# The second context is split on VectorE, and SyncE issues constants, two contexts and the first keys ahead of its loop

## The chip, the cores and the metric

The kernel runs on one core of one Trainium2 chip. The metric is device microseconds of one execution, lower is better. Times are shown as the median of several executions of the same program.

## The reference, cut to what matters

Sixteen independent batches of 128 rows by 256 columns go through two cross attentions and two feed-forward blocks. Keys and values of both attentions are the same array, the context.

```python
x = x + _L0_xattn_ref(_layernorm(x), ctx, ctx)      # 16 heads of 16, causal, 128 queries by 128 keys
x = x + _L0_ffn_ref(_layernorm(x), base_w, base_b, router_w, router_b, lora_A, lora_B)
x = x + _L1_xattn_ref(_layernorm(x), ctx, ctx, gamma)  # 8 heads over the columns, 256 by 256
x = x + _L1_ffn_ref(_layernorm(x), w1, w2, gamma)    # two quantised 256x1024 products, GELU between
```

## The kernel before, in words

The kernel is a software pipeline over the 16 batches. A batch b passes numbered stages, and iteration t of an engine does stage s of batch t - s. Every engine has its own order of stages within an iteration: `fill` for t below 8, `body` for t up to 15 (from 14 on in a hardware loop), `drain` after. The engines meet at semaphores only, and each engine, the DMA-issuing SyncE too, works strictly in its written order, so that a wait holds all that stands behind it.

Scores are computed in bf16 with float32 accuracy. For this every context b is split into high, middle and low bf16 parts in the one buffer `k_split` (four instructions: cast of the high part written twice, subtract into `k_rest`, cast of the middle part, subtract of the low part; each counts `k_split_step` up by one, four to a batch). SyncE stores `k_split` to DRAM (`k_parts`, 512 KB, `store_k`, L655), waits until that has landed (`k_parts_out`), and loads it back in another layout into `k0` (`load_k0`, two DMAs, L616 and L617). The normalised x is split and turned in the same way: ScalarE normalises, GpSimd makes the three parts (`q0_rest`, `q0_mid`, `q0_low`), TensorE transposes (`turn_q0`, L1284), ScalarE copies to `q0_t` (`copy_q0`, L1568), SyncE stores (`store_q0`, L664, 256 KB) and loads (`load_q0`, L616 and L617). TensorE then computes the scores (L1104, L1108), VectorE takes the row maxima (L1801), these are split, transposed, copied and stored by SyncE as two more rows of `q0` (`rows0`, L728), and TensorE computes the transposed scores with the maximum subtracted (L1122, L1126), from which ScalarE takes the exponential.

Context 0 is split by VectorE ahead of its iterations (`split_k0`, L2156 to L2160), all others by GpSimd (`k_high` through the helper at L817, `k_rest_` L833, `k_mid` L817, `k_low` L848). `k_high` of batch b stands in GpSimd's iteration b + 1, ahead of `q0_low` of that iteration, and waits until the keys of batch b - 1 have landed in DRAM.

SyncE's order in the first iterations: `load_x` groups 0 and 1 (L599); t = 0: `load_kv(0)` (L634), `store_q0(0)`; t = 1: `load_kv(1)`, `store_k(0)`, `load_q0(0)`, `load_k0(0)`, `store_q0(1)`; t = 2: `load_kv(2)`, `store_k(1)`, `load_q0(1)`, `rows0(0)`, `load_k0(1)`, `store_q0(2)`; t = 3 the same with all batches one further. ScalarE issues the other groups of x and, at the end of its iteration 2, six constants (L1676): the feed-forward weights `wff_sb` (392 KB), four vectors repeated to all partitions (128, 128, 4 and 0.5 KB) and `lora_b_sb` (128 KB). They are first needed by `x1b_`, `ff` and `logits_` of batch 0.

Of the kernel before, what the change touches and what calls it, by code (L numbers as in the profile page):

```python
# [22 lines left out]
ALU = mybir.AluOpType  # L23
# [4 lines left out]
P = 128  # L28
D = 256
# [28 lines left out]
K_LO, K_HI, K_AGAIN, K_MI = range(SLOTS)  # L58
# [136 lines left out]


X_ITERATIONS = {0: 2, 1: 3, 3: 4, 5: 5}
W_FF_ITERATION = 2
W_LOADS = {4: 0, 6: 1}
W_BATCH = 9 - FF  # L200

# [24 lines left out]
def later(b, n):  # L226

    return not isinstance(b, int) or b >= n


def bank_of(order, user):
# [49 lines left out]
def program(nc, x, kv, w_ff, base_b, router_b, lora_b, attn_gamma, w1, w2, mlp_gamma, out):  # L281
    with ExitStack() as ctx:
# [25 lines left out]
        wff_sb = sb("wff_sb", [P, FT, NFF])  # L308
        lora_b_sb = sb("lora_b_sb", [ER, D])
        base_b_all = sb("base_b_all", [P, D])  # L310
        router_b_all = sb("router_b_all", [P, NE])
        attn_gamma_all = sb("attn_gamma_all", [P, 1])
        mlp_gamma_all = sb("mlp_gamma_all", [P, D])
# [10 lines left out]
        kv_in = sb("kv_in", [P, 2, 2, D])  # L324
        v1_in = sb("v1_in", [P, 2, D])
        k_split = sb("k_split", [P, 2, SLOTS, D], BF16)
        k_rest = sb("k_rest", [P, 2, D])
# [235 lines left out]
        def iterations(engine, fill, body, drain):  # L563
            held.clear()
            for t in range(0, FILL):
                fill(t, t % 2)
            for t in range(FILL, LOOP[0]):
                body(t, t % 2)
            with engine.Fori(0, (LOOP[1] - LOOP[0]) // 2) as turn:
                body(turn * 2 + LOOP[0], LOOP[0] % 2)  # L570
                body(turn * 2 + (LOOP[0] + 1), (LOOP[0] + 1) % 2)
            for order, banks in ((S_BANKS, 2), (ST_BANKS, 2), (T_BANK, 1), (U_BANK, 1), (UT_BANK, 1)):
                for n in range(banks):
                    user, stage = [u for m, u in enumerate(order) if m % banks == n][-1]
                    held[(order[0][0], n)] = ((freed[user], NB - stage),)
            for t in range(LOOP[1], END):
                drain(t, t % 2)
# [17 lines left out]
        def load_x(engine, n):  # L595
            first, end = X_GROUPS[n]
            if n > 2:
                engine.wait_ge(x_late_landed, (n - 2) * 16)
            engine.dma_start(xs[:, first * D:end * D].rearrange("p (b d) -> p b d", d=D),  # L599
                             x[first:end].rearrange("b p d -> p b d")).then_inc(x_landed[n] if n < 2 else x_late_landed, 16)  # L600

        def plain(engine):

            engine.sem_inc(waited, 1)
# [16 lines left out]
        def _(sp):  # L621
            def load_kv(t, odd):
                b, odd = at(t, LOAD_KV), (odd + LOAD_KV) % 2
                if b is None:
                    return
                if later(b, 2):
                    split, placed, landed = b * 4 - 4, b - 1, b * 16 - 16
                    sp.wait_ge(k_split_step, split)
                    plain(sp)
                    sp.wait_ge(v0_placed, placed)  # L630
                    plain(sp)
                    sp.wait_ge(kv_landed, landed)
                    plain(sp)
                sp.dma_start(kv_in[:, odd, :, :], kv[b]).then_inc(kv_landed if later(b, 1) else kv0_landed, 16)  # L634

            def load_v1(t, odd):
                b, odd = at(t, LOAD_V1), (odd + LOAD_V1) % 2
# [10 lines left out]

            def store_k(t):
                b = at(t, STORE_K)  # L650
                if b is None:
                    return
                sp.wait_ge(k_split_step, b * 4 + 4)
                plain(sp)
                sp.dma_start(k_parts[b].rearrange("l p c -> p l c"),  # L655
                             k_split[:, :, :, :].rearrange("p l t c -> p l (t c)")).then_inc(k_parts_out, 16)

# [127 lines left out]
                store_out(t)  # L785

            load_x(sp, 0)
            load_x(sp, 1)
            iterations(sp, fill, body, drain)
            sp.wait_ge(stored, NB * 16)  # L790

# [2 lines left out]
        def _(pool):  # L794
# [23 lines left out]

            def k_high(t, odd):
                b, odd = at(t, K_HIGH), (odd + K_HIGH) % 2  # L820
                if b is None or isinstance(b, int) and b == 0:
                    return
                pool.wait_ge(kv_landed, b * 16)
                pool.wait_ge(k_parts_out, b * 16)
                cast(k_split[:, :, K_HI:K_AGAIN + 1, :],
                     kv_in[:, odd, :, :].unsqueeze(2).broadcast_to([P, 2, 2, D])).then_inc(k_split_step, 1)

            def k_rest_(t, odd):
                b, odd = at(t, K_REST), (odd + K_REST) % 2
                if b is None or isinstance(b, int) and b == 0:  # L830
                    return
                pool.wait_ge(k_split_step, b * 4 + 1)
                pool.tensor_tensor(k_rest[:, :, :], kv_in[:, odd, :, :], k_split[:, :, K_HI, :],  # L833
                                   ALU.subtract).then_inc(k_split_step, 1)

            def k_mid(t):
                b = at(t, K_MID)
                if b is None or isinstance(b, int) and b == 0:
                    return
                pool.wait_ge(k_split_step, b * 4 + 2)  # L840
                cast(k_split[:, :, K_MI, :], k_rest[:, :, :]).then_inc(k_split_step, 1)

            def k_low(t):
                b = at(t, K_LOW)
                if b is None or isinstance(b, int) and b == 0:
                    return
                pool.wait_ge(k_split_step, b * 4 + 3)
                pool.tensor_tensor(k_split[:, :, K_LO, :], k_rest[:, :, :], k_split[:, :, K_MI, :],  # L848
                                   ALU.subtract).then_inc(k_split_step, 1)
# [639 lines left out]
        def _(act):  # L1489
# [151 lines left out]
            def fill(t, odd):  # L1641
                exp1(t, 1)
                norm2_high(t)
                copy_max0(t)
                exp1(t, 5)
                exp2(t)
                copy_max1(t)
                copy_u0(t)
                norm2(t)
                exp1(t, 4)  # L1650
                copy_gated(t)
                exp0(t, 1)
                exp1(t, 6)
                exp0(t, 2)
                copy_q0(t)
                norm1(t)
                exp1(t, 2)
                copy_xh1(t)
                exp1(t, 0)
                norm0(t)  # L1660
                norm0_high(t)
                exp0(t, 3)
                copy_u1(t)
                exp1(t, 3)
                exp0(t, 0)
                exp1(t, 7)
                if t in X_ITERATIONS:
                    load_x(act, X_ITERATIONS[t])
                if t == W_FF_ITERATION:
                    for dst, src in ((base_b_all[:, :], base_b.partition_broadcast(P)),  # L1670
                                     (wff_sb[:, :, :], w_ff.rearrange("(k p) n -> p k n", p=P)),
                                     (lora_b_sb[:, :], lora_b),
                                     (router_b_all[:, :], router_b.partition_broadcast(P)),
                                     (attn_gamma_all[:, :], attn_gamma.partition_broadcast(P)),
                                     (mlp_gamma_all[:, :], mlp_gamma.partition_broadcast(P))):
                        act.dma_start(dst, src).then_inc(weights_in, 16)  # L1676
                if t in W_LOADS:
                    load_weight(W_LOADS[t])

# [119 lines left out]
        def _(dve):  # L1799
# [349 lines left out]
                if isinstance(t, int) and t == 13:  # L2149
                    clip_weight(1, (w1_q, w2_q)[1], (w1_sb, w2_sb)[1])  # L2150

            def split_k0():

                dve.wait_ge(kv0_landed, 16)
                step = Steps(dve, k_split_step, 0, 4)
                step.done(dve.tensor_copy(k_split[:, :, K_HI:K_AGAIN + 1, :],  # L2156
                                          kv_in[:, 0, :, :].unsqueeze(2).broadcast_to([P, 2, 2, D]))).wait()
                step.done(dve.tensor_tensor(k_rest[:, :, :], kv_in[:, 0, :, :], k_split[:, :, K_HI, :], ALU.subtract)).wait()
                step.done(dve.tensor_copy(k_split[:, :, K_MI, :], k_rest[:, :, :])).wait()
                step.done(dve.tensor_tensor(k_split[:, :, K_LO, :], k_rest[:, :, :], k_split[:, :, K_MI, :], ALU.subtract))  # L2160

# [2 lines left out]
                dve.memset(tile[:], 0.0).then_inc(prepared, 1)  # L2164
            dve.memset(v0[:, :, :, :], 1.0).then_inc(prepared, 1)
            stats0_group(0)
            split_k0()
            stats0_group(1)
            dve.memset(k0[STK:STM, :, :].bitcast(F32), ONES_BF16).then_inc(prepared, 1)
            dve.memset(v1[:, :, :], 1.0).then_inc(prepared, 1)  # L2170
            stats0_group(2)
            def stats3_(t):
                b = at(t, STATS3)
                if b is None:
# [168 lines left out]
```

## Time and profile before

| | |
|---|---|
| median of 3 runs | 412.84 us |
| lowest, highest | 410.18, 413.76 us |
| the profiled execution's own time | 415.81 us |
| its span from first to last instruction | 413.4 us |
| busy share of PE, DVE, ACT, POOL | 77%, 74%, 64%, 56% |

PE is TensorE, DVE VectorE, ACT ScalarE, POOL GpSimd, SP SyncE; a q behind the name is the engine's sequencer, which issues DMAs. All positions below are microseconds from the start of the profiled execution's span. The profiled execution lies 2.97 us above the median, and its span 2.4 us below its own time.

### The profile page before, as it was taken

To read this page: it belongs to the slowest core of one execution; us is meant where nothing else is said; L and a number is where in the kernel's file an instruction comes from. 1 tells how busy PE (TensorE), PEld (TensorE's weight loads), DVE (VectorE), ACT (ScalarE), POOL (GpSimd) and SP (SyncE) were. 2 spreads that over 40 slices of the span, in tenths; PEclk is the share of its full clock that TensorE was granted. 3 is DMA by queue.
4 is the path that set the end of the run, shared out by engine and by line. 5 is a ranking of instruction groups with operands and counts; after the bars stand their busy time and mean duration, and the time that the engine had idled before them with its cause. 6 is when DMAs were issued, how large, how long until landed. Compare 5 with 4: busy or idle time off the path is not lost.

```text
span 413.4 us, 9678 instructions
## 1 busy us (share of the span) xinstructions
PE 318.2 (77%) x3010; PEld 192.7 (47%) x3010; DVE 307.9 (74%) x838; ACT 264.4 (64%) x501; POOL 230.9 (56%) x449
## 2 busy tenths in 40 slices
PE   0047366497799899999999999999787578566883
PEld 0024244264465465665655665665443234234453
DVE  6432362759899687889997978897885574999983
ACT  2124153355577488789777876777465347988993
POOL 6257465838585557769656676235424113566534
PEclk9996796888899899999999999999996789999999
DMA  3675774976655738658757577623413400001111
GB/s 101 203 210 131 223 212 105 271 204 168 169 152 172 219 86 237 187 167 225 201 159 212 147 209 193 166 57 92 108 57 94 90 2 1 2 17 36 39 52 63
DMA packets 73137, 56.20 MB, mean 136 GB/s; under 512 B 5376, under 2 KB 62592, under 8 KB 73088
## 3 DMA queue, kind: packets, MB, share of 16 engines
q1 hardware_dynamic: 68896, 50.87, 44.8%
q10 hardware_dynamic: 4192, 4.73, 4.5%
q8 instruction: 24, 0.39, 0.5%
q14 instruction: 25, 0.20, 0.2%
HBM read 36.45 MB, written 18.87 MB: 134 GB/s over the span
## 4 chain that ended last, share of the span: by engine, by line
PE 45%; DMA 16%; DVE 12%; issue 9%; ACT 8%; SPq 6%; POOL 3%; ACTq 0%; POOLq 0%; DVEq 0%
DMA q<-max_t 8%; PE ps_u L1186 6%; PE ps_st L1155 6%; PE ps_s L1140 5%; DMA k<-k_parts 5%; PE ps_ff L1256 4%; PE ps_st L1122 3%; PE ps_st L1126 3%; PE ps_u L1169 3%; DVE max L1801 3%; PE ps_s L1104 2%; PE ps_t L1284 2%; PE ps_s L1108 2%; SPq L616 2%; DMA k_parts<-k_split 2%
## 5 line engine op out<-in xcount | busy, mean ns | idle before, releaser
L1801 DVE TENSOR_REDUCE max<-ps_s 128x2 f32<-128x512 f32 (+1 forms) x192 | 127.1, 685 | 49.0 <-PE ps_s L1108 28.0
L1507 ACT ACTIVATE p<-ps_st 128x512 f32<-128x512 f32 x128 | 71.9, 596 | 23.6 <-PE ps_st L1155 15.6
L1497 ACT ACTIVATE p<-ps_st 128x512 f32<-128x512 f32 x64 | 37.2, 597 | 30.3 <-PE ps_st L1126 29.9
L1140 PE MATMUL ps_s<-k,q 96*128 96x256 bf16 x256 | 51.2, 284 | 5.6 <-DMA k<-k_parts 3.2
L1155 PE MATMUL ps_st<-q,k 98*128 98x256 bf16 x256 | 48.0, 288 | 4.9 <-ACT p L1507 3.1
L1186 PE MATMUL ps_u<-p,v 128*32 128x256 f32 x512 | 39.5, 422 | 3.4 <-POOL v L874 3.4
L1122 PE MATMUL ps_st<-mask_k,ident_bf 128*128 128x512 bf16 x64 | 26.9, 421 | 18.3 <-DMA q<-max_t 17.5
L1155 PEld LDWEIGHTS ps_st<-q,k 98*128 98x128 bf16 x256 | 21.8, 102 | 20.9 <-issue 6.4
L1140 PEld LDWEIGHTS ps_s<-k,q 96*128 96x128 bf16 x256 | 20.3, 100 | 22.8 <-issue 10.9
L923 POOL TENSOR_SCALAR var<-mv 128x1 f32<-128x1 f32 x32 | 7.3, 229 | 41.8 <-DVE mv L1890 34.1
L1284 PE MATMUL ps_t<-ident_bf,q_split 128*128 128x128 bf16 x128 | 12.8, 259 | 21.6 <-POOL q_split L897 21.6
L817 POOL TENSOR_SCALAR k_split<-kv_in 128x1024 bf16<-128x1024 f32 x15 | 15.7, 1049 | 24.2 <-DMA k_parts<-k_split 20.1
L1256 PE MATMUL ps_ff<-wff_sb,xh_t 128*128 128x392 f32 x64 | 27.5, 556 | 2.0 <-DVE w_mean L2048 1.6
L1126 PE MATMUL ps_st<-q,k 98*128 98x128 bf16 x256 | 27.3, 233 | 0.0
L1104 PE MATMUL ps_s<-mask_q,ident_bf 128*128 128x512 bf16 x64 | 25.7, 401 | 1.7 <-DMA k<-k_parts 1.7
L1126 PEld LDWEIGHTS ps_st<-q,k 98*128 98x128 bf16 x256 | 21.7, 105 | 11.1 <-issue 3.5
L1511 ACT ACTIVATE xh<-xs,shift,rstd 128x256 f32<-128x256 f32 x32 | 19.2, 601 | 11.9 <-POOL shift L926 7.8
L1108 PE MATMUL ps_s<-k,q 96*128 96x128 bf16 x256 | 26.0, 226 | 0.0
L1568 ACT COPY q_t<-ps_t 128x1024 bf16<-128x1024 bf16 x16 | 16.1, 1006 | 15.1 <-PE ps_t L1284 15.1
L1169 PE MATMUL ps_u<-p,v 128*32 128x128 f32 x512 | 25.5, 292 | 0.0
L1027 POOL TENSOR_SCALAR amax_c<-amax,rms 128x1 f32<-128x1 f32 x16 | 4.9, 307 | 36.6 <-DVE amax L2203 35.9
L1108 PEld LDWEIGHTS ps_s<-k,q 96*128 96x128 bf16 x256 | 20.7, 101 | 8.7 <-issue 1.4
(147 smaller groups left out, 798.3 us busy)
## 6 DMA issues: line engine op xcount, KB each, us to landing
k_parts<-k_split SPq DMA_DIRECT2D x16, 512.0 KB, 4.1
q<-q_parts SPq DMA_DIRECT2D x32, 256.0 KB, 3.8
k<-k_parts SPq DMA_DIRECT2D x32, 256.0 KB, 3.6
kv_in<-in_kv SPq DMA_DIRECT2D x16, 256.0 KB, 3.7
q_parts<-q_t SPq DMA_DIRECT2D x16, 256.0 KB, 3.7
q<-q_parts SPq DMA_DIRECT2D x32, 128.0 KB, 3.9
k<-k_parts SPq DMA_DIRECT2D x32, 128.0 KB, 3.6
q_parts<-q_split SPq DMA_DIRECT2D x16, 256.0 KB, 2.8
```

Source lines behind the costliest of these rows:

```text
L1104: pe.matmul(out_[:, :], ident_bf[:, :], mask_q[:, :, :].rearrange("p g k -> p (g k)"), start=True, stop=False, skip_group_check=True)
L1108: last = pe.matmul(out_[:, j * P:(j + 1) * P], q0[0:STK, odd, c:c + P], k0[0:STK, odd, c:c + P], start=False, stop=(j == G - 1), skip_grou ...
L1122: pe.matmul(out_[:, :], ident_bf[:, :], mask_k[:, :, :].rearrange("p g k -> p (g k)"), start=True, stop=False, skip_group_check=True)
L1126: last = pe.matmul(out_[:, j * P:(j + 1) * P], k0[0:STM, odd, c:c + P], q0[0:STM, odd, c:c + P], start=False, stop=(j == G - 1), skip_grou ...
L1140: last = pe.matmul(out_[:, f * D:(f + 1) * D], q1[0:STK, odd, h * D + f * P:h * D + (f + 1) * P], k1[0:STK, odd, h * D:(h + 1) * D], start ...
L1155: last = pe.matmul(out_[:, f * D:(f + 1) * D], k1[0:STM, odd, h * D + f * P:h * D + (f + 1) * P], q1[0:STM, odd, h * D:(h + 1) * D], start ...
L1169: last = pe.matmul(ps_u[32 * j:32 * j + 32, g * P:(g + 1) * P], v0[:, odd, h, :], p0[:, g, j * P:(j + 1) * P], start=True, stop=True, skip ...
L1186: last = pe.matmul(ps_u[32 * j:32 * j + 32, g * D:(g + 1) * D], v1[:, f * H1 + h, :], p1[:, h, f * D:(f + 1) * D], start=(f == first), sto ...
L1256: last = pe.matmul(ps_ff[:, 0:NFF], xh1_t[:, f, :], wff_sb[:, f, :], start=(f == 0), stop=(f == FT - 1), skip_group_check=True)
L1497: act.activation(p0[:, g, :], ps_st[bank_of(ST_BANKS, f"s0t{g}")][:, :], ACT.Exp, scale=SCALE).then_inc(exp0_done[g], 1)
L1507: act.activation(p1[:, h, :], ps_st[bank_of(ST_BANKS, f"s1t{h}")][:, :], ACT.Exp, scale=SCALE).then_inc(exp1_done[h], 1)
L1801: dve.tensor_reduce(out_, src, AX.X, ALU.max, negate=True).then_inc(done, 1)
```

## The change

VectorE splits context 1 too, ahead of its iterations, behind the statistics of x group 2, and GpSimd starts with context 2. SyncE, ahead of its iterations, issues x group 0, context 0, x group 1, context 1; waits for context 0; issues three constants; waits for the four split steps of context 0; stores the keys of batch 0; issues the other three constants. Its iterations leave out `load_kv` of batches 0 and 1 and `store_k` of batch 0, and ScalarE no longer issues constants. `split_k(1)` waits for context 1 and for the store of the first keys out of the same buffer. The `memset` of `v1` moves behind `split_k(1)`.

```diff
-W_FF_ITERATION = 2
+def among_first(b, n):
+    return isinstance(b, int) and b < n
...
             def load_kv(t, odd):
                 b, odd = at(t, LOAD_KV), (odd + LOAD_KV) % 2
-                if b is None:
-                    return
-                if later(b, 2):
...
-                sp.dma_start(kv_in[:, odd, :, :], kv[b]).then_inc(kv_landed if later(b, 1) else kv0_landed, 16)
+                if b is None or among_first(b, 2):
+                    return
...
+                sp.dma_start(kv_in[:, odd, :, :], kv[b]).then_inc(kv_landed, 16)
...
             def store_k(t):
                 b = at(t, STORE_K)
-                if b is None:
+                if b is None or among_first(b, 1):
                     return
                 sp.wait_ge(k_split_step, b * 4 + 4)
                 plain(sp)
+                send_k(b)
...
             load_x(sp, 0)
+            sp.dma_start(kv_in[:, 0, :, :], kv[0]).then_inc(kv0_landed, 16)
             load_x(sp, 1)
+            sp.dma_start(kv_in[:, 1, :, :], kv[1]).then_inc(kv_landed, 16)
+            sp.wait_ge(kv0_landed, 16)
+            load_constant(base_b_all[:, :], base_b.partition_broadcast(P))
+            load_constant(wff_sb[:, :, :], w_ff.rearrange("(k p) n -> p k n", p=P))
+            load_constant(router_b_all[:, :], router_b.partition_broadcast(P))
+            sp.wait_ge(k_split_step, 4)
+            send_k(0)
+            load_constant(lora_b_sb[:, :], lora_b)
+            load_constant(attn_gamma_all[:, :], attn_gamma.partition_broadcast(P))
+            load_constant(mlp_gamma_all[:, :], mlp_gamma.partition_broadcast(P))
             iterations(sp, fill, body, drain)
...
             def k_high(t, odd):
-                if b is None or isinstance(b, int) and b == 0:
+                if b is None or among_first(b, 2):
                     return
...
-                if t == W_FF_ITERATION:
-                    for dst, src in ((base_b_all[:, :], base_b.partition_broadcast(P)),
...
-                        act.dma_start(dst, src).then_inc(weights_in, 16)
...
-            def split_k0():
+            def split_k(b):
-                dve.wait_ge(kv0_landed, 16)
-                step = Steps(dve, k_split_step, 0, 4)
+                dve.wait_ge((kv0_landed, kv_landed)[b], 16)
+                if b == 1:
+                    dve.wait_ge(k_parts_out, 16)
+                step = Steps(dve, k_split_step, b, 4)
...
             stats0_group(0)
-            split_k0()
+            split_k(0)
             stats0_group(1)
             dve.memset(k0[STK:STM, :, :].bitcast(F32), ONES_BF16).then_inc(prepared, 1)
+            stats0_group(2)
+            split_k(1)
             dve.memset(v1[:, :, :], 1.0).then_inc(prepared, 1)
-            stats0_group(2)
```

`k_rest_`, `k_mid` and `k_low` leave out batch 1 in the same way as `k_high`.

## Rows read from the trace of the kernel before

**Rows 1.** The page's head: the span and the number of instructions.
```profile
span 413.4 us, 9678 instructions
```
**Rows 2.** Windows: start:end, length, busy of each engine (instructions), granted clock, DMA share, GB/s.
```profile
12.00:25.00 13.00, 1.06 (x9) 0.80 (x10) 2.78 (x5) 2.04 (x4) 6.17 (x12) 1.00 0.71 203
25.00:34.00 9.00, 4.01 (x22) 2.26 (x23) 3.11 (x6) 0.98 (x3) 4.84 (x8) 0.89 0.84 238
34.00:50.00 16.00, 9.17 (x88) 5.62 (x88) 6.34 (x19) 5.12 (x9) 7.53 (x12) 0.71 0.71 194
...
112.00:352.00 240.00, 217.40 (x2144) 129.44 (x2142) 195.92 (x551) 170.56 (x333) 132.61 (x248) 0.95 0.52 141
```
**Rows 3.** Chain of waits that ended last, 0 to 70: start, length, what.
```profile
12.79 7.96 DMA k_parts<-k_split
...
21.48 3.45 DMA k<-k_parts
...
30.43 0.60 SPq L728
...
31.07 2.70 DMA q<-max_t
...
37.75 4.13 DMA q_parts<-q_t
...
44.30 5.13 DMA q<-max_t
```
**Rows 4.** Timeline, DMA issues: start, length, engine, line, what.
```profile
1.62 0.43 SPq L634 DMA_DIRECT2D kv_in<-in_kv  x1
...
11.87 0.33 SPq L664 DMA_DIRECT2D q_parts<-q_t  x1
...
12.79 0.38 SPq L655 DMA_DIRECT2D k_parts<-k_split  x1
...
13.37 1.21 ACTq L1676 DMA_DIRECT2D attn_gamma_all<-in_attn_gamma  x1
...
17.26 0.69 SPq L616 DMA_DIRECT2D q<-q_parts  x1
18.01 0.61 SPq L617 DMA_DIRECT2D q<-q_parts  x1
20.83 0.60 SPq L616 DMA_DIRECT2D k<-k_parts  x1
...
24.02 0.39 ACTq L599 DMA_DIRECT2D xs<-in_x  x1
```
**Rows 5.** Timeline of VectorE and GpSimd in the first 13 us.
```profile
4.72 0.69 DVE L2156 CAST k_split<-kv_in 128x1024 bf16<-128x1024 f32 x1 [1.02 <-DMA kv_in<-in_kv]
4.88 0.58 POOL L937 TENSOR_TENSOR mean<-mv,rstd 128x1 f32<-128x1 f32 x1
...
5.66 0.53 POOL L939 TENSOR_SCALAR shift<-mean 128x1 f32<-128x1 f32 x1 [0.20 <-POOL mean L937]
...
6.64 0.69 DVE L2160 TENSOR_TENSOR k_split<-k_rest,k_split 128x512 bf16<-128x512 f32 x1
...
10.62 0.19 POOL L937 TENSOR_TENSOR mean<-mv,rstd 128x1 f32<-128x1 f32 x1
...
12.31 1.76 DVE L2062 MEMSET k<- 2x2048 f32 x1 [0.48 <-issue]
```
**Rows 6.** Timeline: GpSimd behind the landing of the first keys, VectorE's first maxima.
```profile
20.92 1.04 POOL L817 TENSOR_SCALAR k_split<-kv_in 128x1024 bf16<-128x1024 f32 x1 [5.95 <-DMA k_parts<-k_split]
...
26.05 0.69 DVE L1801 TENSOR_REDUCE max<-ps_s 128x4 f32<-128x512 f32 x1 [10.86 <-PE ps_s L1108]
```
**Rows 7.** Lines L664 (q_parts) and L655 (k_parts), first 120 us, seven DMAs each.
```profile
DMA to landing us min/median/max: 2.0/3.1/5.3
...
DMA to landing us min/median/max: 4.0/4.7/8.2
```
**Rows 8.** DMA view, 10 to 26 us: GB/s in 40 equal slices.
```profile
GB/s 0 0 0 0 0 0 15 61 23 51 110 162 167 201 253 363 398 394 401 414 384 389 367 328 349 263 211 119 95 70 101 278 288 214 105 12 0 26 18 18
```

More of the change, by code:

```diff
@@ L623, in load_kv, with load_constant @@
                 b, odd = at(t, LOAD_KV), (odd + LOAD_KV) % 2
-                if b is None:
+                if b is None or among_first(b, 2):
                     return
-                if later(b, 2):
[L627 to L633, printed above, removed]
-                sp.dma_start(kv_in[:, odd, :, :], kv[b]).then_inc(kv_landed if later(b, 1) else kv0_landed, 16)
+                split, placed, landed = b * 4 - 4, b - 1, b * 16 - 16
+                sp.wait_ge(k_split_step, split)
+                plain(sp)
+                sp.wait_ge(v0_placed, placed)
+                plain(sp)
+                sp.wait_ge(kv_landed, landed)
+                plain(sp)
+                sp.dma_start(kv_in[:, odd, :, :], kv[b]).then_inc(kv_landed, 16)
+            def load_constant(dst, src):
+                sp.dma_start(dst, src).then_inc(weights_in, 16)
             def load_v1(t, odd):
@@ L654, in store_k, with send_k @@
                 plain(sp)
+                send_k(b)
+            def send_k(b):
                 sp.dma_start(k_parts[b].rearrange("l p c -> p l c"),
@@ L829, in k_rest_ @@
                 b, odd = at(t, K_REST), (odd + K_REST) % 2
-                if b is None or isinstance(b, int) and b == 0:
+                if b is None or among_first(b, 2):
                     return
@@ L837, in k_mid @@
                 b = at(t, K_MID)
-                if b is None or isinstance(b, int) and b == 0:
+                if b is None or among_first(b, 2):
                     return
@@ L844, in k_low @@
                 b = at(t, K_LOW)
-                if b is None or isinstance(b, int) and b == 0:
+                if b is None or among_first(b, 2):
                     return
@@ L1668, in fill @@
                     load_x(act, X_ITERATIONS[t])
-                if t == W_FF_ITERATION:
-                    for dst, src in ((base_b_all[:, :], base_b.partition_broadcast(P)),
[L1671 to L1675, printed above, removed]
-                        act.dma_start(dst, src).then_inc(weights_in, 16)
                 if t in W_LOADS:
@@ L2150, in body @@
                     clip_weight(1, (w1_q, w2_q)[1], (w1_sb, w2_sb)[1])
-            def split_k0():
-                dve.wait_ge(kv0_landed, 16)
-                step = Steps(dve, k_split_step, 0, 4)
+            def split_k(b):
[3 more added lines that the diff above has]
+                step = Steps(dve, k_split_step, b, 4)
                 step.done(dve.tensor_copy(k_split[:, :, K_HI:K_AGAIN + 1, :],
-                                          kv_in[:, 0, :, :].unsqueeze(2).broadcast_to([P, 2, 2, D]))).wait()
-                step.done(dve.tensor_tensor(k_rest[:, :, :], kv_in[:, 0, :, :], k_split[:, :, K_HI, :], ALU.subtract)).wait()
+                                          kv_in[:, b, :, :].unsqueeze(2).broadcast_to([P, 2, 2, D]))).wait()
+                step.done(dve.tensor_tensor(k_rest[:, :, :], kv_in[:, b, :, :], k_split[:, :, K_HI, :], ALU.subtract)).wait()
                 step.done(dve.tensor_copy(k_split[:, :, K_MI, :], k_rest[:, :, :])).wait()
```

## The prediction

> **What bounds the kernel now.** I read the page's head first: a span of 413.4 us [rows 1]. The windows by stage come next. In the loop (112 to 352 us) TensorE is busy for 217.40 of 240 us, so that part is bound by work that the change doesn't touch. At the start it is different: from 12 to 25 us TensorE is busy for 1.06 of 13 us, and even from 34 to 50 for only 9.17 of 16 [rows 2]. There the kernel waits. The change lies wholly in the first 25 us, so the question is what ends the wait there, and whether what it gives is kept to the end.
>
> The chain of waits names it: store of the first keys 7.96 us, from 12.79; load of the keys 3.45 us from its second issue at 21.48, landed at 24.93, with the first scores right behind; rows of the maxima issued at 30.43 and landing 2.70 us after 31.07; then q of batch 2 stored for 4.13 us, and the next rows of maxima for 5.13 [rows 3]. The reader is to see two things. First, the start of the pipeline is a chain of DMA round trips through one in-order issuer. Second, from 31 us on the chain goes through work that hangs on the batch before it, so a start that is earlier by some time should shift all the rest by that time.
>
> The timeline of issues shows how the start is made up. The first q is stored at 11.87, the first keys at 12.79 although their split ended at 7.33 (6.64 + 0.69), because SyncE stands at `store_q0(0)` meanwhile [rows 4, 5]. The q loads go out at 17.26, when the q store has landed 5.3 us after its issue, and end at 18.62. SyncE then stands until 20.83 for the keys [rows 4, 7]. In the same 9 us the DMA engines carry the constants, context 1, q and keys together, at up to 414 GB/s [rows 8].
>
> **The change part by part.**
>
> *Keys of batch 0 sent early.* Context 0 is issued one 0.43 us issue earlier (the first x group alone stands ahead of it) [rows 4], so `split_k(0)` ends near 6.9. The store of the keys goes out near 7.0 instead of 12.79. It can land after 4.0 to 8.2 us [rows 7], by 11.0 to 15.2. I take 4.7, 11.7. SyncE will ask for it only behind the q loads, see below, near 15.4. So the wait from 18.62 to 20.83 goes: **2.2 us**. Even the slowest landing shown costs nothing here.
>
> *Constants moved out of the q store's way.* Six DMAs, 0.8 MB, leave ScalarE and go to SyncE, three from about 4.3, when context 0 has landed, three from 7.4. On SyncE each costs its issue: 1.21 us for the dearest [rows 4]; so at most 3.6 us for the last three. They end by 11.0, ahead of `store_q0(0)`, which waits for q until 11.4 anyway: price nothing, and if that cover were gone up to 3.6 us. ScalarE gains its issue time, worth nothing, since it idles then (2.04 of 13 us busy) [rows 2]. The worth is in the DMA engines: most of the 1.8 MB that crowded 12 to 21 us (constants 0.8, context 1 and q 0.25 each, keys 0.5) is now through by about 12. The q store took 5.3 us in that crowd, and its smallest is 2.0, its median in the first 120 us 3.1 [rows 7]. Bounds of the gain are 3.3 and 0. The store meets at most the tail of the last constants, so I take 2.7 us to landing: **2.6 us**.
>
> *The q chain itself.* GpSimd's mean and shift of x group 0 took 0.58 and 0.53 us while VectorE split context 0, against 0.19 for the same mean later; each ended 0.05 us behind a VectorE instruction [rows 5]. With the split 0.4 us earlier they end 0.4 us earlier, and q is stored at 11.45. Bounds: 0 (context 0 lands no earlier) and 0.45. I take **0.4 us**.
>
> *The k load has a new neighbour.* ScalarE issues x group 4 (512 KB) at its iteration 3, right after copying q of batch 1. That stood at 24.02, when the first k load was all but landed [rows 4]. Now GpSimd is free, so q of batch 1 is there near 17 and x group 4 goes out near 17.3, a microsecond behind the second k issue at 16.3. At some 400 GB/s [rows 8] its 512 KB are worth 1.3 us if all of it came ahead. Bounds 0 and 1.3, I take **0.4 us lost**, since only its first part can interleave.
>
> *Context 1 on VectorE.* Four instructions, 2.61 us as for context 0 (4.72 to 7.33) [rows 5], from about 11.7 to 14.3. VectorE has room: behind it stand the memset of `v1`, that of `k1` (1.76 us) and one group of statistics, done by about 18.3, while the first maxima are due near 21.2 (26.05 less the gain) [rows 5, 6]. Price nothing; the cover is 2.9 us wide. From GpSimd it takes 3.96 us of work and above all the 5.95 us wait at `k_high(1)` [rows 6], behind which `q0_low(1)`, the turn and the copy of q of batch 1 stood. The store of that q was at SyncE's fill end behind the k loads anyway; now it leaves near 17.9 instead of 24.8. It is needed when `load_q0(1)`, which stands ahead of `rows0(0)` on SyncE, is issued. `rows0(0)` is due at 20.1 + 5.5 = 25.6 (30.43 less 24.93 is 5.5 [rows 3]). The q store of batch 1 lands by 17.9 + 4.1 = 22.0, the load is issued by 23.4: 2.2 us of slack. So the freed GpSimd yields nothing by itself, but without it this queue would eat the whole gain.
>
> The trace shows that a VectorE split holds up GpSimd (0.58 against 0.19 us) [rows 5]. The Trainium skill, "SBUF — State Buffer", section "Who interferes with whom", says that the two share a port pair as an exclusive lock and the second to issue fully blocks. By that rule the new split could hold GpSimd's parts of q of batch 1 for its whole length, 2.6 us.
>
> Priced from rows: `store_q0(1)` at 20.5 instead of 17.9, its load issued by 26.0, `rows0(0)` 0.4 us late. I count nothing and keep 0.4 us in the range; from a delay of 2.2 us it costs at all.
>
> *Check of the path.* q stored 11.45, landed 14.15, q loads issued to 15.5 (1.36 us as from 17.26 to 18.62), two k issues to 16.3 for the start of the second, 3.45 + 0.4 to landing: 20.15. Before 24.93. The sum is 2.2 + 2.6 + 0.4 - 0.4 = **4.8 us**.
>
> *What is late next.* The rows of maxima land 2.70 us after their issue, about as now. The next batches' keys and q are all in place before they are asked for, since SyncE takes them in the same order behind `store_q0(2)`. From 34 us on I see no resource with a date of its own: the w1 and w2 loads and the later x groups are issued by iterations that shift too. So 4.8 us is kept. From the span that makes 408.6; the profiled execution is 2.97 us above the median, and I take the difference off the median: 412.84 - 4.8 = **408.0 us**.
>
> **The rivals.**
>
> *A. The q store is not faster.* If the fixed part of its landing or the last constants still hold it for 4.5 to 5.3 us, only the key wait and a bit of the chain go: 1.5 to 3.5 us, say 2.4, **410.4 us**. For it: the q store at 37.75 took 4.13 us with less around it than at 12 us [rows 3]. Against: the 2.0 us in quiet stretches [rows 7].
>
> *B. The transfer was hidden anyway, or the gain is given back.* The fill is a chain of waits for DMAs whose landing varies between 2.7 and 5.1 us for the same two rows of maxima [rows 3]. One such row landing 2.4 us later in two iterations gives all back: **412.8 us**. For it: the pattern of collisions with the 1 MB weight loads may change. Against: those are issued by the same chain, so they shift alike. The Trainium skill, "DMA: Bandwidth & Descriptors", section "Issuing engines are not separate DMA queues", holds that all issuers end on the same 16 engines, so moving the constants from ScalarE to SyncE would by itself bring nothing; only their earlier time counts.
>
> *C. Slower.* TensorE's granted clock in the loop falls. It is 0.95 there, 0.71 from 34 to 50 us [rows 2], so it does move between its levels, 1.2 and 2.4 GHz. TensorE's 217.4 us at 0.89 (the value of 25 to 34 us) would take 14.7 us more, less 4.8: **422.7 us**. It makes the kernel over 1% slower from a granted clock of about 0.91 down. Against: the loop's work and its order are the same.
>
> **How the numbers follow.** Forecast (4.1 to 6.5 us gained): 0.50. A: 0.28. B: 0.12. C: 0.06. More than 6.5 us, where the k load isn't disturbed and the rows of maxima land faster too: 0.04. A measurement here tells about 1% from no change, 4.1 us, which is a bound through the middle of my cases: faster 0.54, within 1% 0.39, slower 0.07. The range that leaves out no more than 2 in 10 reaches from the upper bounds of the terms (3.3 + 2.2 + 0.45 and 1 us at the rows: 7 us, 405.8) to the better half of B, 412.2. The forecast's own range is 406.3 to 408.7.
>
> **What would show it.** Key store issued near 7.0 and landed before 13; q store near 11.45, landing in 2 to 3.1 us; no gap between the q loads and the k loads on SyncE; first scores near 20.2; first maxima there without VectorE being late; the second issue of the rows of maxima near 26.3; 34 to 112 us of before found again 4.8 us earlier; granted clock in the loop 0.95. I am wrong if the q store lands no faster, if `split_k(1)` starts after 15, if `load_q0(1)` holds `rows0(0)`, or if the shift shrinks between 26 and 112 us.

## The result and the profile after

The changed kernel takes 407.56 us (median of 20 runs, 402.08 to 413.54), the kernel before 414.39 us in the same comparison (20 runs). The ratio is 0.9844, 95% interval 0.9814 to 0.9874: faster by 1.6%. Some executions of either kernel are slower as a whole by a per cent or more; the medians include these, the ratios here and below leave them out. Two later comparisons of the same two kernels gave 0.9874 [0.9814, 0.9933] and 0.9893 [0.9846, 0.9940], so 1.1 to 1.6%, or 4.4 to 6.4 us of some 412. The profiled span went from 413.4 to 405.6 us. Of these 7.8 us some 1.4 are the profiled execution of before itself, whose own time of 415.81 lies that much above the median of 414.39.

The chain of waits that ended last, changed kernel, 0 to 70 us (start, length, what). It answers [rows 3].

```profile
12.20 2.02 DMA q_parts<-q_t
...
16.42 4.30 DMA k<-k_parts
...
26.21 0.60 SPq L737
...
26.85 1.73 DMA q<-max_t
...
38.53 5.58 DMA q<-max_t
...
53.56 7.31 DMA q<-max_t
```

The store of the keys is gone from the chain. The store of the first q stands there instead, with 2.02 us. The first keys are loaded by 20.72 (16.42 + 4.30) instead of 24.93: 4.2 us earlier. The rows of maxima of batch 0 have landed at 28.58 instead of 33.77, 5.2 us earlier, since they took 1.73 instead of 2.70 us.

SyncE's issues, changed kernel (timeline). They answer [rows 4].

```profile
4.59 0.33 SPq L640 DMA_DIRECT2D base_b_all<-in_base_b  x1
...
7.23 0.38 SPq L664 DMA_DIRECT2D k_parts<-k_split  x1
...
8.64 1.19 SPq L640 DMA_DIRECT2D mlp_gamma_all<-in_mlp_gamma  x1
...
12.20 0.33 SPq L673 DMA_DIRECT2D q_parts<-q_t  x1
...
14.30 0.70 SPq L620 DMA_DIRECT2D q<-q_parts  x1
15.05 0.61 SPq L621 DMA_DIRECT2D q<-q_parts  x1
15.77 0.60 SPq L620 DMA_DIRECT2D k<-k_parts  x1
16.42 0.61 SPq L621 DMA_DIRECT2D k<-k_parts  x1
```

The last constant is out at 9.83, the q store goes out at 12.20, 0.33 us later than before (11.87), and the four loads follow each other without a gap.

GpSimd and VectorE in the first 15 us, changed kernel (timeline). They answer [rows 5].

```profile
4.23 1.09 POOL L955 TENSOR_TENSOR rstd<-var,neg_half 128x1 f32<-128x1 f32 x1
4.60 0.69 DVE L2170 CAST k_split<-kv_in 128x1024 bf16<-128x1024 f32 x1 [0.90 <-DMA kv_in<-in_kv]
5.41 0.66 POOL L957 TENSOR_TENSOR mean<-mv,rstd 128x1 f32<-128x1 f32 x1
...
11.96 0.69 DVE L2170 CAST k_split<-kv_in 128x1024 bf16<-128x1024 f32 x1 [0.73 <-DMA k_parts<-k_split]
...
13.86 0.66 POOL L902 TENSOR_TENSOR rest<-xh,q_split 128x256 f32<-128x256 f32 x1
13.88 1.19 DVE L2174 TENSOR_TENSOR k_split<-k_rest,k_split 128x512 bf16<-128x512 f32 x1
```

The split of context 0 begins 0.12 us earlier than before (4.60 against 4.72), not 0.4. It now meets GpSimd's rstd as well, which takes 1.09 us. The split of context 1 begins at 11.96, when the first keys have landed.

The windows by stage, changed kernel, answering [rows 2]: busy of PE, PEld, DVE, ACT, POOL, granted clock, DMA share, GB/s. The loop of before (112 to 352) is taken 5 us earlier.

```profile
12.00:25.00 13.00, 4.73 (x28) 2.83 (x28) 8.81 (x14) 3.10 (x6) 4.96 (x9) 1.00 0.73 205
25.00:34.00 9.00, 5.51 (x38) 3.50 (x39) 0.67 (x4) 3.45 (x6) 6.73 (x11) 0.65 0.42 115
...
107.00:347.00 240.00, 216.22 (x2141) 128.82 (x2138) 197.82 (x554) 171.62 (x336) 132.14 (x250) 0.95 0.51 139
```

The loop is as it was, at a granted clock of 0.95 as before. TensorE starts inside the first window now.

### The profile page after: what moved, and what is told of

Same layout as the page of the kernel before. It is cut to its first block, busy times and chain, and to the rows that moved or that the text cites. A ratio compares the mean times of both kernels' runs of the same rounds, so it can differ in the third digit from the quotient of the medians.

```text
span 405.6 us, 9676 instructions
## 1 busy us (share of the span) xinstructions
PE 317.0 (78%) x3010; PEld 192.5 (47%) x3010; DVE 314.3 (77%) x842; ACT 264.5 (65%) x501; POOL 228.1 (56%) x445
## 4 chain that ended last, share of the span: by engine, by line
PE 45%; DVE 20%; DMA 10%; ACT 9%; issue 9%; POOL 3%; SPq 2%; ACTq 0%; POOLq 0%; DVEq 0%
DMA q<-max_t 6%; PE ps_u L1206 6%; PE ps_st L1175 6%; PE ps_s L1160 5%; DVE max L1813 5%; PE ps_ff L1276 4%; PE ps_st L1142 4%; PE ps_st L1146 3%; PE ps_u L1189 3%; DMA k<-k_parts 3%; PE ps_s L1124 3%; PE ps_s L1128 3%; ACT hr L1758 2%; DVE amax L2236 2%; ACT p L1527 2%
## 5 line engine op out<-in xcount | busy, mean ns | idle before, releaser
L1142 PE MATMUL ps_st<-mask_k,ident_bf 128*128 128x512 bf16 x64 | 27.9, 435 | 15.3 <-DMA q<-max_t 14.6
L1146 PE MATMUL ps_st<-q,k 98*128 98x128 bf16 x256 | 28.2, 239 | 0.0
L1276 PE MATMUL ps_ff<-wff_sb,xh_t 128*128 128x392 f32 x64 | 26.2, 533 | 2.0 <-DVE w_mean L2060 1.6
L837 POOL TENSOR_SCALAR k_split<-kv_in 128x1024 bf16<-128x1024 f32 x14 | 14.7, 1050 | 16.8 <-DMA k_parts<-k_split 15.4
L1206 PEld LDWEIGHTS ps_u<-p,v 128*32 128x32 f32 x512 | 13.5, 115 | 19.5 <-issue 11.7
```

The lines of the kernel that those rows point to most:

```text
L1142: pe.matmul(out_[:, :], ident_bf[:, :], mask_k[:, :, :].rearrange("p g k -> p (g k)"), start=True, stop=False, skip_group_check=True)
L1146: last = pe.matmul(out_[:, j * P:(j + 1) * P], k0[0:STM, odd, c:c + P], q0[0:STM, odd, c:c + P], start=False, stop=(j == G - 1), skip_grou ...
L1206: last = pe.matmul(ps_u[32 * j:32 * j + 32, g * D:(g + 1) * D], v1[:, f * H1 + h, :], p1[:, h, f * D:(f + 1) * D], start=(f == first), sto ...
L1276: last = pe.matmul(ps_ff[:, 0:NFF], xh1_t[:, f, :], wff_sb[:, f, :], start=(f == 0), stop=(f == FT - 1), skip_group_check=True)
```

## The experiments

The change has four parts: contexts early, constants early, keys of batch 0 early, context 1 on VectorE. All kernels below load the contexts early except the one that says otherwise. Times are ratios to the kernel before on the same chip, with 95% intervals. "Keys loaded" is where the second load of `k0` of batch 0 has landed, in the profile.

### The whole change again, and its parts

`e1_after` is the changed kernel.

> The changed kernel as it is, beside the parts. My theory (three terms on the chain to the first scores: wait for the keys, landing of the first q store, and what happens to q's own chain): first scores near 20.7 us of the profile, total 1.2 to 1.8% below before. A rival (the profile after had a lucky run of landings behind 60 us) expects the same first scores and a total only 1.0% below.

Measured: 0.9874 [0.9814, 0.9933], keys loaded at 20.25 (16.21 + 4.04). The total is in line with the theory; the interval does not exclude the rival's 1.0%.

`e2_keys_early` puts the constants back and gives context 1 back to GpSimd:

```diff
-            load_constant(base_b_all[:, :], base_b.partition_broadcast(P))
...
+                if t == 2:
+                    for dst, src in (...):
+                        act.dma_start(dst, src).then_inc(weights_in, 16)
...
-            split_k(1)
```

> Only the early contexts and the early store of the first keys: the six constants are back on ScalarE at its iteration 2, context 1 is split by GpSimd. My theory: the q store of batch 0 meets the constants again and lands in about 4 us instead of 2.0, so first scores near 22 us, total about 3 us (0.7%) below before. Rival (the constants cost nothing where they were): first scores near 20.7, total as the changed kernel. Rival (the gain is GpSimd's freedom from its 5.95 us wait): that wait is gone here too, since the keys land by 12, so again the total of the changed kernel.

Measured: 1.0035 [0.9990, 1.0080]. Nothing is gained at all, which none of the three expected. The chain of waits of this kernel:

```profile
12.03 4.20 DMA q_parts<-q_t
...
18.42 7.51 DMA k<-k_parts
25.98 0.61 PE ps_s L1118
```

The q store took 4.20 us, as my theory said, and the second load of the keys was issued at 18.42, 3.1 us earlier than before. But it took 7.51 us instead of 3.45. The early store of the keys has a second effect: GpSimd no longer waits for it, q of batch 1 is copied 6 us earlier, and with it goes whatever is issued behind that copy.

```profile
17.72 0.39 ACTq L603 DMA_DIRECT2D xs<-in_x  x1
```

This is x group 4 in this kernel's timeline, 512 KB, 0.70 us ahead of the second load of the keys.

`e6_keys_x4_late` is that kernel with x group 4 one iteration later:

```diff
-X_ITERATIONS = {0: 2, 1: 3, 3: 4, 5: 5}
+X_ITERATIONS = {0: 2, 1: 3, 4: 4, 5: 5}
```

> The kernel of e2_keys_early with one constant changed: ScalarE loads x group 4 (512 KB) in its iteration 4 instead of 3. There the second load of the first keys took 7.51 us, issued at 18.42. Theory 1 (it shares the DMA engines with x group 4, issued at 17.7): it lands in about 4 us, first scores near 22.5, total 2 to 3 us less than there. Theory 2 (it is held by SyncE's own stores and context load behind it, issued from 19.1 on, or by the constants issued before 14.5): it still takes over 6.5 us and first scores stay near 25.

The chain of waits:

```profile
12.12 4.49 DMA q_parts<-q_t
...
18.80 3.78 DMA k<-k_parts
22.63 0.61 PE ps_s L1118
```

Theory 1 holds for the load: 3.78 us instead of 7.51, with SyncE's own q store, context load and key store behind it as before (19.52 to 21.04). So x group 4 was the cost. The first scores now start at 22.63, 2.3 us earlier than before (24.97). The total did not follow: 1.0000 [0.9958, 1.0041]. `rows0` ran 2.4 us ahead of before at its first issue, 3.4 at its second, but 0.5 at its third, behind the place where x group 4 (37.21) now meets the weight load of w1 (37.63). What happens later I can't assign: the profiled execution took 416.62 us, 2.8 above the median of its kernel (413.87), so its later positions can't be set beside those of before.

`e3_consts_early` sends only the constants early. The keys are stored in iteration 1, GpSimd splits context 1:

```diff
-            sp.wait_ge(k_split_step, 4)
-            send_k(0)
...
             def store_k(t):
-                if b is None or among_first(b, 1):
+                if b is None:
...
-            split_k(1)
```

> Only the constants and contexts early: the first keys are stored by SyncE in its iteration 1 behind the q store, as before, and context 1 is split by GpSimd. My theory: the keys leave at 12.7, land near 17.2, so first scores near 21.5 us and 3.4 us below before (0.8%); the two parts overlap, they don't add up. Rival (the early key store is what matters): no more than 1 us below before.

Measured: 0.9900 [0.9832, 0.9967], keys loaded at 20.18 (16.27 + 3.91), as early as with the whole change. The DMA view of this kernel, 12 to 14 us (KB each, us to landing):

```profile
k_parts<-k_split SPq DMA_DIRECT2D x1, 512.0 KB, 3.0
q_parts<-q_t SPq DMA_DIRECT2D x1, 256.0 KB, 2.1
```

The keys left at 12.47, as late as before (12.79), and landed by 15.5 instead of 20.75, just before SyncE asked for them at 15.62. The rival, that the early store is what matters, falls, and so does a term of my sum.

`e4_pool_split` is the changed kernel with context 1 on GpSimd (the last line of the diff above, and GpSimd's four stages from batch 1 on).

> The changed kernel with context 1 split by GpSimd again, all else early. My theory: the split on VectorE is no part of the gain, GpSimd finds the buffer free when it comes to it; first scores near 20.7, store of the second keys up to 1 us later, total within 0.3% of the changed kernel. Rival (the split on VectorE carries the gain): 1% slower than the changed kernel.

Measured: 0.9797 [0.9731, 0.9862], keys loaded at 20.17; the second keys left at 19.99 instead of 19.38. Beside the 0.9874 of the changed kernel in the same comparison this is not slower, so the rival's 1% slower is excluded; the intervals are too wide to confirm my 0.3%.

`e5_split_only` has VectorE's split alone; constants and keys leave where they left before.

> Only the split of context 1 on VectorE (and the contexts loaded early): constants on ScalarE at its iteration 2, first keys stored by SyncE in its iteration 1. My theory: no gain. The first keys land near 20.8 or, with context 1 gone from the crowd, 1 us sooner; VectorE then stands at the split until they land, and its own first maxima come behind it, a memset and statistics, up to 1.3 us late. Total within 0.5% of before. Rival (the split on VectorE carries the gain, by ending GpSimd's 5.95 us wait): 1% below before or more.

Measured: 1.0005 [0.9961, 1.0049]. In its chain of waits:

```profile
12.58 7.51 DMA k_parts<-k_split
20.82 6.95 DMA k<-k_parts
```

The first scores began at 27.82, 2.9 us later than before. VectorE was not what was late: it had finished its statistics at 26.8 and then waited 2.12 us for scores. The load of the keys was late again, 6.95 us. X group 4 had left at 17.34, since GpSimd was free early here too, and was in flight for 8.4 us, until 25.7; that it is the cause here as in `e2_keys_early` is likely and was not tried. The total is unchanged all the same. The rows of maxima left 2.9 us later than before at their first issue (33.33 against 30.43) and only 0.2 us later at 144.84 (144.66): the fill made up for the late start.

### Where the constants may stand

`e9_consts_t3` is the kernel before, contexts included, with one number changed:

```diff
-W_FF_ITERATION = 2
+W_FF_ITERATION = 3
```

> The kernel before with one number changed: ScalarE issues the six constants at the end of its iteration 3 instead of 2, behind x group 4. Theory (what counts is that the constants are out of the first round trips; earlier or later is the same there): the first q store lands in 2 to 3 us, the first keys in 3 to 4, first scores near 21 instead of 24.9, and then part of it is given back, since the constants now meet the second q store, the second keys and the rows of maxima from 20 to 30 us: 1 to 3 us below before in total. Rival (they must be through before the first q store; behind it they only move the crowd): within 0.3% of before or slower.

Measured: 0.9986 [0.9886, 1.0086]. Its timeline and, for the last line, its chain of waits show how the start is won and lost:

```profile
11.92 0.33 SPq L664 DMA_DIRECT2D q_parts<-q_t  x1
...
14.03 0.69 SPq L616 DMA_DIRECT2D q<-q_parts  x1
...
20.52 0.53 ACTq L1676 DMA_DIRECT2D base_b_all<-in_base_b  x1
20.92 0.34 SPq L664 DMA_DIRECT2D q_parts<-q_t  x1
...
26.80 0.58 SPq L616 DMA_DIRECT2D q<-q_parts  x1
27.43 0.62 SPq L617 DMA_DIRECT2D q<-q_parts  x1
28.10 1.23 SPq L728 DMA_DIRECT2D q<-max_t  x2
```

```profile
28.74 4.73 DMA q<-max_t
```

The first q store landed in 2.1 us and the first maxima began at 22.04, 4.0 us earlier than before: for the first scores a later place does nearly as well as an earlier one. But the second q store, issued 0.4 us behind the first constant, took 5.8 us. Its load stands ahead of the rows of maxima on SyncE and holds them until 28.10, though they had been copied at 26.46, and then they land in 4.73 us. At 33.47 all of the 4 us but 0.3 is gone (33.77 before). My theory was right for the start. In total the interval of 1% either way decides between neither theory nor rival; the rival's "within 0.3%" fits what the rows of maxima show at 33.47.

### The other terms of the sum

`e7_split0_later` makes VectorE wait until GpSimd's four small operations are done:

```diff
             def split_k(b):
+                if b == 0:
+                    dve.wait_ge(rstd0_step, 4)
```

> The changed kernel, VectorE waits with the split of context 0 until GpSimd has done the four small operations of x group 0. My theory (in the changed kernel VectorE's split holds GpSimd: rstd 1.09 us against 0.58, mean 0.66 against 0.19): the four operations end near 5.5 instead of 6.5, the first q is stored near 11.2 instead of 12.2, first scores about 0.8 us earlier, total about 0.8 us less than the changed kernel; the store of the first keys moves to about 8.1, which nobody asks for before 15. Rival (the hold only moves to GpSimd's later operations on q): q stored at 12.0 or later, nothing gained.

GpSimd in this kernel:

```profile
4.29 0.57 POOL L955 TENSOR_TENSOR rstd<-var,neg_half 128x1 f32<-128x1 f32 x1
4.93 0.19 POOL L957 TENSOR_TENSOR mean<-mv,rstd 128x1 f32<-128x1 f32 x1
...
8.28 0.97 POOL L917 TENSOR_TENSOR q_split<-rest,q_split 128x256 bf16<-128x256 f32 x1
```

The hold is gone from rstd and mean (0.57 and 0.19 us) and returns in part on q's low half (0.97 instead of 0.67). The q store went out at 11.56, 0.6 us earlier than in the changed kernel, but it took 3.17 us instead of 2.02 and landed at 14.73, later than the 14.22 of the changed kernel. Total 0.9857 [0.9800, 0.9914], no difference. A miss. SyncE was not what was late, it had been free since 11.07. But the keys, issued at 8.76 instead of 7.23, pushed the last constants back, and the last of these (128 KB, issued at 10.58) takes 3.5 us to land and so was in flight beside the q store for 2.5 us, against 1.0 us in the changed kernel. I take that for the cause; no run tries it.

`e12_after_x4_late` is the changed kernel with x group 4 one iteration later, the same edit as in `e6_keys_x4_late`.

> The changed kernel, with x group 4 (512 KB) loaded by ScalarE in its iteration 4 instead of 3. If x group 4 is what made the second load of the first keys 4.30 us instead of 3.45: it lands in 3.5 us, first scores near 19.9, and x group 4 then meets the weight load of w1 near 33 us. In total within 1 us of the changed kernel, since the same bytes only crowd another round trip. Rival (the slower key load is due to something else): 4.0 us or more again.

Measured: 0.9882 [0.9837, 0.9927]. The key load took 3.97 us (16.18 to 20.15), within 0.12 us of the 4.04 and 4.09 of two other profiles of the changed kernel. So x group 4, which in the changed kernel leaves 1.1 us behind the second key load (17.52 against 16.42), costs at most a few tenths; the rival is right. What makes it 4.0 instead of 3.45 was not tested. A rival that I had not named is the load of q, issued just ahead on the same queue: where the second key load leaves 1.4 us behind the second q load, it took 3.78 to 4.30 us in the eight profiles in which x group 4 is not ahead of it; where it leaves 3.5 us behind (before) or 2.8 us (`e9_consts_t3`, 17.57 against 14.78), it took 3.45 and 3.4 us. In its new place x group 4 is dear:

```profile
16.18 3.97 DMA k<-k_parts
...
38.47 8.05 DMA q<-max_t
```

The second line is two DMAs of 4 KB, beside 512 KB of x and 1 MB of w1 issued by ScalarE from 35.12 to 37.22, and behind the q load of SyncE itself, against 5.58 us in the changed kernel, where the 512 KB of x are missing.

### A version that goes further

`e8_k_load_first` puts the load of the first keys ahead of that of the first q. The keys have long landed, and SyncE only waits there.

```diff
             def fill(t, odd):
...
                 load_v1(t, odd)
+                if t == 1:
+                    load_k0(t, odd)
                 load_q0(t, odd)
                 rows0(t, odd)
-                load_k0(t, odd)
+                if t != 1:
+                    load_k0(t, odd)
```

> The changed kernel, SyncE issues the load of the first keys ahead of the load of the first q, right behind the q store, instead of behind the q loads. My theory (the first scores hang on the second of two round trips in a row, q store and then two loads issued one after the other): keys load at 12.6 and lands by 17, q loads at 14.3 and 15.0 and the last lands near 19; first scores near 19 instead of 20.7, total 1.5 us less than the changed kernel. Rival (the keys' load crowds the q store, issued 0.4 us before it): q store lands 1 us later or more, first scores near 20.5, no gain.

Its chain of waits:

```profile
11.97 2.05 DMA q_parts<-q_t
...
14.75 3.78 DMA q<-q_parts
18.66 0.58 PE ps_s L1127
```

The q store is not disturbed by the 384 KB issued behind it (2.05 us), and the first scores start at 18.66 instead of 20.77. Measured: 0.9796 [0.9719, 0.9873]. Since this interval overlaps that of the changed kernel, both ran once more on one chip.

> The changed kernel again, to stand beside the next one on the same chip: 1.3 to 1.6% below before.

> The kernel of e8_k_load_first again, beside the changed kernel on one chip. If its first scores, 2.1 us earlier than in the changed kernel, are kept to the end: 1.8 to 2.1% below before, 0.5% below the changed kernel. If what is won at the first scores is lost in later landings: the time of the changed kernel.

Measured side by side: the changed kernel 0.9893 [0.9846, 0.9940], the reordered one 0.9774 [0.9700, 0.9848], with first scores 1.5 us apart, not 2.1 (maxima from 21.51 and 19.96). Both comparisons give the reordered kernel about 2% below before, 0.5 to 1.2% below the changed kernel. That it is faster than before is measured; that it beats the changed kernel is likely, the intervals just touch. The 1.2% between the two is more than 1.5 us at the first scores explain; the rest I can't assign.

## Why the prediction was right, and where it was not

**The number.** 408.0 us was forecast, 407.56 measured. The stage, the chain and the side on which it ends were right, and the first scores came 4.2 to 4.7 us earlier in three profiles of the changed kernel, against a sum of 4.8. Two things in this are luck. I took the 4.8 us off a median of 412.84 us, and in the comparison the kernel before had 414.39: the medians are 6.8 us apart, so the time was hit more closely than the gain. And within the sum an error of 0.7 us at the q store, which gained more, hides one of 0.7 us at the q chain, which lost; the k load's 0.45 us more lost is most of what is left.

**Keys of batch 0 sent early, 2.2 us.** This step failed, though the 2.2 us did go. In `e3_consts_early` the keys leave late and the wait is gone too, since they land in 3.0 us. Both "terms", the 5.3 us of the q store and the 7.96 us of the keys, come from one thing, the crowd of 1.8 MB [rows 8], and taking the 0.8 MB of constants out of it mends both. With the constants gone the early store adds nothing that shows; without that it brings the first scores 2.3 us forward (`e6_keys_x4_late`), but neither there nor in `e2_keys_early` did it bring anything in total. I had read two waits in a row as two causes.

**Constants out of the way, 2.6 us.** Right cause, sized too small: the store took 2.02 us instead of 5.3, so 3.3. It is more than the term: it carries the change. The profile of `e9_consts_t3` adds what I had not said: the new place must be empty as well, and of the two that were tried the one ahead of the first q store is. The Trainium skill, "DMA: Bandwidth & Descriptors", section "Issuing engines are not separate DMA queues", says that all DMAs run on the same 16 DMA engines and interleave there, whichever engine issued them. These runs agree: x group 4, issued by ScalarE, made a load issued by SyncE take 7.51 us instead of 3.78. Whether the constants would do as well if ScalarE issued them early is not shown, since no run issued them from ScalarE before the first q store.

**The q chain, 0.4 us gained.** Wrong in sign: 0.33 us lost. I took context 0 to land as much earlier as it is issued. It landed 0.12 us earlier, just enough for VectorE's first cast to catch GpSimd's rstd.

**The k load beside x group 4, 0.4 us lost.** The loss was 0.85 us (4.30 against 3.45; 0.6 in the two other profiles), and `e12_after_x4_late` shows that at most a small part of it is x group 4's. In `e2_keys_early`, where x group 4 leaves 0.7 us ahead instead of 1.1 us behind, the same neighbour costs 3.7 us.

**Context 1 on VectorE, nothing.** Right that it costs and brings nothing (`e5_split_only`, `e4_pool_split`), wrong in the reason I gave for keeping it: without it the queue does not eat the gain. The second keys leave 0.6 us later and nobody waits. It held GpSimd up (the mean of x group 2 took 0.66 us instead of 0.19), by 0.8 us in all from 11.91 to 15.4, not by the 2.6 us of the whole split; q of batch 1 was stored at 18.32, within the slack.

**What is late next.** I kept the landing of the rows of maxima as it was. It was 1.73 us instead of 2.70 in the profile (1.74 and 1.73 in the two others), which makes 5.2 us at 28.6. From there to the end the profiles of one and the same kernel part: measured against before, the changed kernel's rows of maxima ran 6.8, 5.5 and 7.3 us ahead at the fifth issue and 6.7, 6.1 and 4.7 at 241 us. The measured 6.8 us between the medians is 1.6 more than the 5.2, and this I can't assign; it lies within that scatter.

**Is the gain at the start kept?** I had said that a start that is earlier by some time should shift all the rest by that time. The runs don't bear this out as a rule. `e5_split_only` started 2.9 us late and `e6_keys_x4_late` 2.3 us early, and both ended with the time of before. Every kernel with the constants early, with its first scores 3.9 us or more ahead, gained 1.0% or more in its measured ratio, and no other kernel gained anything that shows. Whether the first scores count or the emptier stretch behind them, no run takes apart: `e9_consts_t3` had early first scores without early constants and lost them again, but its total is known to 1% only.

**The rivals.** A (q store not faster) is refuted by 2.02 us. C (clock) did not happen, 0.95 in the loop. B is the instructive one: it did not happen in the changed kernel but in `e2_keys_early` and `e9_consts_t3`, where 3.1 us (at the issue of the keys' load) and 4.0 us (at the first maxima) are given back within the next two long DMAs, and in `e6_keys_x4_late`, where 3.4 us at the second rows of maxima were 0.5 at the third and the rest of the course stays open.

## What to carry to other kernels

Where a chain consists of DMA round trips, ask of each long landing what else was in flight, before counting its wait as something to be removed: two long waits in a row can be one crowd. And measure the total too: a start that was 2 to 3 us early or late did not show in it here. Work without a date belongs into a stretch in which the DMA engines idle and which is ahead of the chain; moved behind the first link it found the next one here. And when a step becomes free earlier, list what is issued behind it, since a large transfer that comes 1 us sooner can cost more than the step gains.

## What the runs showed of the hardware

- The same 256 KB store took 2.0 us with the engines nearly empty and 5.3 among 1.8 MB. The loads of the first keys (384 KB in two DMAs) landed 3.5 to 4.3 us behind the issue of their second part, but 7.5 when 512 KB had been issued from the other queue 0.7 us ahead.
- Two DMAs of 4 KB took 8.05 us behind 1.5 MB from the other queue and 384 KB of their own queue, and 1.73 us where the engines moved 27 GB/s on average meanwhile (changed kernel, 26.85 to 28.58).
- GpSimd's rstd began 0.37 us ahead of VectorE's cast and was still the one that was held (1.09 us against 0.57; the cast kept its 0.69). At 13.86 it was the other way round: VectorE's subtract, begun 0.02 us behind a GpSimd subtract of 0.66 us, took 1.19 us instead of 0.69, and the same again in `e1_after` and `e8_k_load_first`. The Trainium skill, "SBUF — State Buffer", section "Who interferes with whom", says that the one that issues first keeps the pair for the whole instruction; the second case agrees with it in who is held, the first does not as the trace shows starts.
